# The last pair of batches of a gated feed-forward layer: another order of its last tiles on TensorE, and batch 6's second tokens through ScalarE and GpSimd

## The reference, cut to what matters

```python
gate = silu(qlinear(layernorm(x), wq_gate, s_gate))
up = qlinear(layernorm(x), wq_up, s_up)
x = x + qlinear(gate * up, wq_down, s_down)   # W = (wq - 128) * scale per output row
```

## Time and profile before

| what | us |
|---|---|
| median of 3 runs | 572.52 (572.25 to 573.15) |
| the profiled execution | 572.94 |
| its span | 571.1 |
| TensorE busy in the span | 560.6 (98%) |
| last matmul of the program ends | 565.93 |
| three last stores issued | 567.08, 567.39, 567.50 |

### The profile page before, as it was taken

One profiled execution on the slowest core, in us unless ns is written; L12 is line 12 of the kernel. 1 busy time (PEld: TensorE's weight loads), 2 busy tenths in 40 slices (PEclk: granted clock), 3 DMA queues, 4 the chain that ended last, 5 costly groups with the idle time before them and its releaser, 6 DMA issues.

```text
span 571.1 us, 12867 instructions
## 1 busy us (share of the span) xinstructions
PE 560.6 (98%) x4135; PEld 530.1 (93%) x4135; DVE 464.1 (81%) x1475; ACT 370.5 (65%) x1037; POOL 210.9 (37%) x316
## 2 busy tenths in 40 slices
PE   8999999999999999999999999999999999999996
PEld 8899999999999999999999999999998899888885
DVE  4888789778977997798789778977887899878875
ACT  5887556656755756666657566756985777754553
POOL 3782224233223332342234223223356677413221
PEclk9999999999999999999999999999999999999999
DMA  8807000000000000000000000000000000001002
GB/s 329 299 1 231 2 1 3 1 1 0 0 0 0 0 0 0 0 0 0 0 0 0 0 0 0 0 0 1 2 1 1 1 2 1 1 1 38 15 23 77
DMA packets 9152, 14.71 MB, mean 26 GB/s; under 512 B 1568, under 2 KB 6688, under 8 KB 9120
## 3 DMA queue, kind: packets, MB, share of 16 engines
q1 hardware_dynamic: 8848, 14.04, 7.0%
q10 hardware_dynamic: 272, 0.26, 0.1%
HBM read 12.20 MB, written 2.10 MB: 25 GB/s over the span
## 4 chain that ended last, share of the span: by engine, by line
PE 91%; DVE 4%; ACT 3%; issue 1%; POOL 0%; DVEq 0%; POOLq 0%
PE bank L647 71%; PE bank L750 5%; PE bank L732 3%; PE bank L657 2%; PE bank L753 2%; PE bank L938 2%; PE bank L926 2%; PE bank L863 1%; PE bank L734 1%; ACT prob L1150 1%; PE bank L1057 1%; ACT big L1123 0%; DVE prob L1562 0%; DVE qT L1508 0%; ACT raw L1346 0%
## 5 line engine op out<-in xcount | busy, mean ns | idle before, releaser
L521 POOL TENSOR_SCALAR prob<-prob,rowinv 128x256 f32<-128x256 f32 (+1 forms) x127 | 96.3, 770 | 267.2 <-DVE rowinv L1578 267.2
L647 PE MATMUL bank<-xT,big 128*128 128x256 f32 x984 | 129.5, 283 | 0.1
L647 PEld LDWEIGHTS bank<-xT,big 128*128 128x128 f32 x984 | 123.2, 191 | 1.0 <-issue 0.2
L1150 ACT ACTIVATE prob<-prob,negmax 128x128 f32<-128x128 f32 (+1 forms) x256 | 112.8, 445 | 8.4 <-DVE negmax L1562 8.4
L647 PE MATMUL bank<-wp,oT 128*128 128x256 f32 x768 | 102.5, 283 | 0.4 <-DVE oT L1508 0.3
L647 PEld LDWEIGHTS bank<-wp,oT 128*128 128x128 f32 x768 | 96.8, 190 | 1.4 <-DVE oT L1508 0.8
L1112 ACT ACTIVATE qT<-bank 128x512 fp32r<-128x512 f32 x68 | 40.6, 597 | 71.5 <-PE bank L647 71.4
L647 PE MATMUL bank<-pT,v 128*128 128x512 f32 (+1 forms) x384 | 79.8, 343 | 0.7 <-DVE pT L1508 0.5
L647 PEld LDWEIGHTS bank<-pT,v 128*128 128x128 f32 x384 | 63.2, 189 | 9.9 <-issue 1.0
L1508 DVE TENSOR_TENSOR pT<-bank,pT 128x512 fp32r<-128x512 f32 (+1 forms) x128 | 65.1, 550 | 3.0 <-ACT pT L1112 2.9
L1112 ACT ACTIVATE pT<-bank 128x512 fp32r<-128x512 f32 (+1 forms) x128 | 55.2, 483 | 13.1 <-PE bank L750 11.0
(11 more groups left out here) (189 smaller groups left out, 990.5 us busy)
## 6 DMA issues: line engine op xcount, KB each, us to landing
raw<-in_wq SPq DMA_DIRECT2D x4, 512.0 KB, 6.5
raw<-in_wp SPq DMA_DIRECT2D x4, 512.0 KB, 6.9
x<-in_x SPq DMA_DIRECT2D x7, 256.0 KB, 6.8
out<-x SPq DMA_DIRECT2D x6, 256.0 KB, 2.1
raw<-in_w_gu SPq DMA_DIRECT2D x2, 640.0 KB, 5.4
raw<-in_w_in SPq DMA_DIRECT2D x1, 768.0 KB, 4.8
raw<-in_w_down SPq DMA_DIRECT2D x1, 640.0 KB, 7.3
raw<-in_wk SPq DMA_DIRECT2D x1, 512.0 KB, 3.9
```

Of the source, the lines that this page charges most:

```text
L521: m = pool.tensor_scalar(prob[:, j % 2, 0, a:b], prob[:, j % 2, 0, a:b], rowinv[:, j % 2, r:r + 1], None, ALU.mult)
L647: m = pe.matmul(out, lhs(a), rhs(b), start=first and i == 0, stop=last and i == len(passes) - 1, skip_group_check=True)
L1150: m = act.activation(prob[:, j % 2, i, a:b], prob[:, j % 2, i, a:b], ACT.Exp, scale=-1.0, bias=negmax[:, 2 * i + r:2 * i + r + 1], accum_o ...
```

## The change

TensorE: after tile 3 of the last pair, tile 4 of both batches is multiplied first, then tile 5 of both. Through the whole last pair, batch 6's second tokens go into bank 0 (`bM[:, 0:D]`) and no longer into the right half of bank 1; their first product starts that bank anew, behind a wait for `s_glo`.

VectorE: it scales only the first tokens of batch 6 before it turns to batch 7. ScalarE: it copies batch 6's second tokens from bank 0 to `scaled[1][:, 1, :]`. GpSimd: in place of one add of 512 columns it adds the first tokens (256 columns), multiplies the copied second tokens by `s_down`, and adds them, each with a wait; ScalarE's store of batch 6 waits for the last, as before.

```diff
+            first, second = (x[:, ST * b + t, :] for t in range(ST))
             pool.wait_ge(s_gsc, b + 1)
-            xs = x[:, ST * b:ST * (b + 1), :]
-            pool.tensor_tensor(xs, xs, scaled[0][:, :, :], ALU.add).then_inc(s_ga, 1)
+            pool.tensor_tensor(first, first, scaled[0][:, 0, :], ALU.add)
+            pool.wait_ge(s_gcopy, 1)
+            pool.tensor_tensor(scaled[1][:, 1, :], scaled[1][:, 1, :], biases[:, 2, :], ALU.mult).then_inc(s_gmul, 1)
+            pool.wait_ge(s_gmul, 1)
+            pool.tensor_tensor(second, second, scaled[1][:, 1, :], ALU.add).then_inc(s_ga, 1)
...
                         pe.wait_ge(s_gsc, 2 * m - 1 + b)
+                        if isinstance(m, int) and m == NB // 2 - 1 and b == 0:
+                            pe.wait_ge(s_glo, NB)
                     for t in range(ST):
                         at = b * S + t * P
+                        room, alone = bD[b][:, t * D:(t + 1) * D], t == 0
+                        if isinstance(m, int) and m == NB // 2 - 1 and b == 0 and t == 1:
+                            room, alone = bM[:, 0:D], True
...
-                for half in range(2):
-                    for i in (HT - 2, HT - 1):
+                for i in (HT - 2, HT - 1):
+                    for half in range(2):
                         down_project(NB // 2 - 1, i, weight_parts, half)
...
             b = NB - 2
+            act.wait_ge(s_gd, b + 1)
+            act.wait_ge(s_ga, b + 2)
+            act.activation(scaled[1][:, 1, :], bM[:, 0:D], ACT.Copy).then_inc(s_gcopy, 1)
             act.wait_ge(s_ga, b + 3)
...
-            scale_down(NB - 2, 0)
+            dve.wait_ge(s_gd, NB - 1)
+            dve.wait_ge(s_ga, NB - 1)
+            dve.tensor_tensor(scaled[0][:, 0, :], bD[0][:, 0:D], biases[:, 2, :], ALU.mult).then_inc(s_gsc, 1)
```

More of the change, by code:

```diff
@@ L296, in build @@
         s_gsc = sem("down_scaled")
+        s_gcopy = sem("second_tokens_of_batch_6_copied")
+        s_gmul = sem("second_tokens_of_batch_6_scaled")
         s_ga = sem("gated_added")
@@ L1026, in down_project @@
                         pe.wait_ge(s_gsc, 2 * m - 1 + b)
+                        if isinstance(m, int) and m == NB // 2 - 1 and b == 0:
+                            pe.wait_ge(s_glo, NB)
                     for t in range(ST):
                         at = b * S + t * P
+                        room, alone = bD[b][:, t * D:(t + 1) * D], t == 0
+                        if isinstance(m, int) and m == NB // 2 - 1 and b == 0 and t == 1:
+                            room, alone = bM[:, 0:D], True
                         if i == HT - 1:
-                            mm = mm3(pe, bD[b][:, t * D:(t + 1) * D], lambda a: hT[i % 3][:, 0, at:at + P],
+                            mm = mm3(pe, room, lambda a: hT[i % 3][:, 0, at:at + P],
                                      lambda a: down[:, a, i, :], False, True, ((0, 0), (0, 1))[:weight_parts])
                         else:
-                            mm = mm3(pe, bD[b][:, t * D:(t + 1) * D], lambda a: hT[i % 3][:, a, at:at + P],
-                                     lambda a: down[:, a, i, :], i == 0 and t == 0, False,
+                            mm = mm3(pe, room, lambda a: hT[i % 3][:, a, at:at + P],
+                                     lambda a: down[:, a, i, :], i == 0 and alone, False,
                                      PASSES if weight_parts == 2 else PASSES[::2])
```

## The result

The changed kernel takes **574.15 us** (median of 20 runs, 572.16 to 574.81), the kernel before 572.53 (20 runs, 571.97 to 573.15). The ratio is 1.0024, 95% interval 1.0018 to 1.0030: slower by 1.6 us, where 572.0 and a range to 573.1 were predicted. The 20 runs are two groups, five at 572.16 to 572.97 and fifteen at 573.76 to 574.81, with nothing between. Before is one group. The profiled execution took 573.97, of the later group, with a span of 572.1. The ratios leave out three executions that were far longer than all others: 621.04 and 913.55 us of the kernel before, beside the experiments, and 1943.72 of one experiment.

The account below looks back on a forecast made before the run. TensorE is busy 98%, but VectorE's path and batch 6's GpSimd and store path bound the tail. Batch 7's stores -0.39, batch 6's issue +0.56, landing 570.3 against 570.8: -0.5, giving 572.0 us, range 571.4 to 573.1.

Parts of the forecast that it names:

- batch 6's products end earlier: TensorE's tail: tile 5 of batch 6 follows sixteen matmuls without a restart, ending at 565.13 instead of 565.23, -0.1.
- batch 7's first store issued: VectorE's tail: one of six operations goes, so this store is issued at 566.69 instead of 567.08, -0.39.
- ScalarE's copy: ScalarE, batch 6's second tokens: 0.38 us, hidden behind GpSimd's first add, cost nothing.
- GpSimd's operations: GpSimd's tail: one add of 1.27 becomes three operations of 256 columns, 0.745 us each.
- batch 6's store issued: ScalarE's queue after GpSimd's last add: issued at 567.95 instead of 567.39, +0.56.
- its landing after the issue: Batch 6's store, now last: 2.35 us, the middle of 2.1 alone and 2.6 with neighbours, landing at 570.3.
- The stores: Final landings: batch 6's store becomes the last, landing at 570.3 against 570.8 before, sum -0.5.
- the 3.3 of the last store: Batch 7's second store before the change: issued 567.50, landing 3.3 later at 570.8, the end to improve on.
- GpSimd did not stretch: Rival: GpSimd's three operations stretch beside VectorE to 926 ns, +0.1 to +0.4, 572.8; chance 0.13.
- The landings rival: Final stores: the surplus in 3.3 belongs to whatever lands last, end stays at 570.65 to 570.95, 572.5; chance 0.22.
- The rival that code had moved: Instruction stream: shifted code adds or removes one stretch on the path, +-0.5, 571.5 or 573.0; chance 0.06.
- The rule on completions across queues: Full-gain rival's support: completions land only after a DMA engine's earlier writes; batch 6's store takes 2.1, -0.75, 571.8; chance 0.2.

Follow-up runs that it names:

- changed, TensorE longer: Changed kernel with twelve unused 128x128 transposes behind TensorE's last product, ahead of its jump over the second program: 573.60 us.
- before, store late: Kernel before with one unused GpSimd multiplication of 128x256 ahead of the last add, so only batch 6's store is issued about 0.8 later: 574.47 us.
- without the second program: TensorE's branch and program for other weights, never run here, left out: kernel before 572.40 us, changed kernel 572.38 us.
- the version of its own: Kernel before with TensorE's new order, GpSimd adding batch 6 in two halves, each stored at once; no own bank, no ScalarE copy: 571.75 us.

## Why the prediction was wrong, point by point

| step | predicted | measured |
|---|---|---|
| batch 6's products end earlier | 0.1 | 0.01 (ScalarE and VectorE start at 564.84 + 0.41 = 565.25, before 565.26; GpSimd 565.76) |
| batch 7's first store issued | 566.69 | 566.78 |
| ScalarE's copy | 0.38, hidden | 0.38, hidden |
| GpSimd's operations | 0.745 each | 0.73, 0.73, 0.72 |
| batch 6's store issued | 567.95 | 568.00 |
| its landing after the issue | 2.35 (2.1 to 2.6, at most 3.3) | 4.1 in the profiled run; 2.2 with no instruction transfer in the way |
| time | 572.0 | 574.15 |

In the first line VectorE's start is the better witness than the modelled end of a matmul. Of the 0.1 almost nothing was there: the prediction let tile 5 follow the sixteen matmuls without a restart and so end earlier, but its first product starts at 564.72 as before, and VectorE 0.53 after that, in before 0.55.

**The step that failed** is the one headed "The stores". It priced the landing by what other stores were in flight and looked at no other user of the DMA engines. The profile's page had one in plain sight: its DMA section lists q8 and q14 of kind "instruction", and the trace has 16 KB of them at 569.92. Its cause is found by the runs: no jump, no transfer (before and after alike) and a landing of 2.2; a jump behind all landings, the same code and again 2.2; a later jump, a later transfer (568.6, 571.5); and in the profiled runs in which the transfer met a store's data, one sixteenth of the store was late, by one packet or by its whole share.

How close store and transfer come orders the landings of the profiled runs. The distance is from batch 6's first data packet to the start of the second transfer:

| kernel | distance, us | packets of the store held until after it | landing | long runs |
|---|---|---|---|---|
| before | 1.55 | 0 | 2.6 | 0 of 20 (1 of 100 beside the experiments) |
| before, new order | 1.33 | 0 | 2.6 | 0 of 11 |
| changed, store by SyncE | 1.20 | 0 | 2.4 | 4 of 11 |
| changed | 1.14 | 1 | 4.1 | 15 of 20 |
| changed, old order | 0.90 | 16 | 4.4 | 9 of 12 |
| changed, TensorE longer | 0.75 | 16 | 4.1 | 6 of 11 |
| before, store late | 0.10 | 16 | 4.2 | 5 of 7 |

A store of 256 KB alone wants about 0.9 us of data time (568.60 to 569.50 without the jump); in before, beside batch 7's second piece, it took 1.5, to 569.90, just ahead of the transfer at 569.92. The change issued the store 0.6 later and brought its first packet 0.4 closer to the transfer. Each row is one profiled run, so the order of the landings is shown and an exact bound is not, and the share of long runs does not follow the distance (15 of 20 at 1.14, 6 of 11 at 0.75). Three things stay open. In before, the changed kernel and the one with the store by SyncE, the transfer begins within 0.01 of the end of the last packet before it, so it may itself have waited for that packet. In the runs with 16 packets held, these had not begun when the transfer did, although the store's first packets were 0.1 to 0.9 us old by then; what held them until then is not seen. And it is not known why a quarter of the changed kernel's runs escape, or what makes the second transfer come 3.1 to 4.0 us behind the first.

**The smaller miss** is the gain itself. I read the 3.3 of the last store in before as the standing price of its end and took 0.5 off it. In 20 runs of before and 11 without the second program the medians differ by 0.1 us, and there the same store took 2.7, so the rest of that 3.3 was this one execution's. With 2.7, before ends at 567.47 + 2.7 = 570.2 and the change at 568.00 + 2.2 = 570.2 (the trace has the issue at 567.47, not 567.50): the same end, as the medians without the jump have it, 572.38 against 572.40.

**The rivals.** GpSimd did not stretch. The landings rival had the place right, "whatever lands last", but its price (570.65 to 570.95) was taken from the 3.3. The rival that code had moved priced 0.5 us for a gap on an engine; in the changed kernel's trace the instructions cost their time on a DMA engine that also carried data. The rule on completions across queues was not tested: the store's own packets are seen to be late. But in the changed kernel's profiled run the last completion lands 0.9 after its packet, in before 0.8, in the other traces 0.3 to 0.6, and what made this difference is open.

The Trainium skill's page "Runtime: NRT & Kernel Launch", section "Instruction fetch mechanics", says that instructions are refilled in blocks of 16 KiB by DMA and that a taken branch to a place outside the window forces such a transfer. The trace agrees on both (16 KB packets on q8; none after 559 us without the jump). That such a block delays a store is what the runs here add.

## What to carry to other kernels

Before pricing a tail that ends in a store, list every transfer in its last 5 us, instructions too, and ask which of them may share the DMA engines with the last one: here a 16 KB block made a landing of 2.2 into one of about 4, with the store's first packet only 0.4 us closer to it. An engine that has finished its work is not out of the way: its jump to the end belongs early, and a wait ahead of it cost 1.6 us here, by its transfer among the stores and by its own 3.3 us together. And make the last store small: batch 6 in two pieces of 128 KB, the first sent when its half is ready, gave 0.6 us against before (2.2 against the changed kernel), and 0.9 in the version of its own, where moving work between engines gave nothing.

## What the runs showed of the hardware that was not expected

- One 16 KB transfer of instructions behind the jump took 0.95 to 1.66 us as a single packet, and up to 16 packets of a store (1 KB each, 0.05 to 0.08 us apiece otherwise) came only after it, though it started as much as 0.9 us after that store's first packets. That they share its DMA engine is inferred.
- The first transfer behind TensorE's jump starts 1.0 to 1.5 us after the last product's operand is ready, and twelve queued transposes (1.47 us) do not hold it up: the branch started at 564.90, the first transpose at 565.18. A semaphore wait ahead of it does (568.6, 571.5).
- The jump over the second program takes TensorE's sequencer 3.3 to 4.2 us. With the jump last, the span ended 3.7 us behind the last landing (570.53 and 574.2).
- The second transfer comes after TensorE is done (569.67 against 568.3 in the changed kernel). Nothing waits for it, and it is the one that delayed the store.
- The same store, 256 KB and last, landed 2.2 us after its issue (2.4 on SyncE's queue) where no such transfer met it and 3.8 to 4.4 where one did, which fits the two groups of run times.
